# Attention maxima split into three parts before the turn instead of after it, in a one-core transformer block

## The reference, cut to what matters

```
q, k, v = layernorm(x) @ w_qkv, split into heads
scores = q k^T / sqrt(8), causal mask (-inf above the diagonal)
scores += head_scale * (q . dir) * (k . dir)
attn = softmax(scores)           # over the keys
x = x + layernorm((attn v) @ w_out)
```

## Time and profile before

| what | us |
|---|---|
| runs | 540.02, 540.23 (median), 547.24 |
| profiled execution, span from first to last instruction | 542.4 |
| TensorE busy | 440.5 (81%) |
| VectorE busy | 329.6 (61%) |
| ScalarE busy | 244.3 (45%) |
| GpSimd busy | 142.2 (26%) |
| mean granted TensorE clock | 0.899 |

### The profile page before, as it was taken

How to read it: one execution, slowest core, us unless ns; L and a number is a source line. 1 busy time by engine, 2 the same in 40 slices (tenths; PEclk the granted TensorE clock), 3 DMA queues, 4 the chain that set the end, 5 groups by cost and what they waited for, 6 DMA issues and landing times. The chain is left out here.

```text
span 542.4 us, 10816 instructions
## 1 busy us (share of the span) xinstructions
PE 440.5 (81%) x3980; PEld 267.0 (49%) x3980; DVE 329.6 (61%) x885; ACT 244.3 (45%) x432; POOL 142.2 (26%) x211
## 2 busy tenths in 40 slices
PE   1845978989898998999898968888699989898800
PEld 0522432434434352434434345645499889888800
DVE  3975956868787876878782764599223322223356
ACT  1520145666665765677675827552122222213330
POOL 9300000010111101011111002424626665573423
PEclk9975576999989997999988988999979999999965
DMA  3065254100202020000000008100447768766352
GB/s 102 21 179 150 78 157 119 58 5 3 60 2 61 2 60 2 2 3 3 3 2 2 1 2 232 39 2 1 160 137 228 205 194 215 215 206 190 98 160 78
DMA packets 44616, 46.60 MB, mean 86 GB/s; under 512 B 6355, under 2 KB 33364, under 8 KB 44564
## 3 DMA queue, kind: packets, MB, share of 16 engines
q1 hardware_dynamic: 42132, 40.92, 25.8%
q0 software_dynamic: 2432, 4.99, 3.6%
HBM read 34.80 MB, written 10.88 MB: 84 GB/s over the span
## 5 line engine op out<-in xcount | busy, mean ns | idle before, releaser
L611 ACT ACTIVATE probs<-banks 128x1024 f32<-128x1024 f32 (+1 forms) x192 | 145.3, 810 | 80.6 <-PE banks L468 52.5
L749 DVE TENSOR_REDUCE mx_part<-banks 128x1 f32<-128x512 f32 (+3 forms) x256 | 133.2, 584 | 42.1 <-PE banks L444 34.2
L444 PE MATMUL banks<-k_st,q_st 48*128 48x512 bf16 (+3 forms) x384 | 123.9, 370 | 14.5 <-DMA k_st<-k_rows 12.3
L461 PE MATMUL banks<-q_st,k_st 51*128 51x512 bf16 (+3 forms) x384 | 103.7, 349 | 17.7 <-DMA q_st<-mx_rows 11.3
L480 PE MATMUL banks<-probs,v_pad 128*32 128x512 f32 (+3 forms) x768 | 86.8, 526 | 0.0
L461 PEld LDWEIGHTS banks<-q_st,k_st 51*128 51x128 bf16 x384 | 32.1, 96 | 75.7 <-ACT probs L611 49.9
L749 DVE TENSOR_REDUCE mx<-banks 128x1 f32<-128x512 f32 (+3 forms) x128 | 54.7, 485 | 20.1 <-PE banks L450 20.0
L1488 DVE TENSOR_TENSOR hidden<-banks,gate 128x512 f32<-128x512 f32 x38 | 26.3, 692 | 61.6 <-ACT gate L1256 28.8
L355 POOL TENSOR_TENSOR mx_rest<-mx_neg,mx_rows 16x128 f32<-16x128 f32 x16 | 6.7, 417 | 199.2 <-ACT mx_neg L621 199.2
L444 PEld LDWEIGHTS banks<-k_st,q_st 48*128 48x128 bf16 x384 | 34.7, 95 | 43.6 <-DVE mx_part L749 24.8
L448 PE MATMUL banks<-mask_qk,ident_half 64*128 64x128 bf16 x256 | 56.2, 232 | 0.0
(11 more groups left out here) (198 smaller groups left out, 616.1 us busy)
## 6 DMA issues: line engine op xcount, KB each, us to landing
w_g<-in_w_gate SPq DMA_DIRECT2D x38, 256.0 KB
w_u<-in_w_up SPq DMA_DIRECT2D x38, 256.0 KB
q_rows<-parts SPq DMA_DIRECT2D x24, 128.0 KB, 2.4
k_rows<-parts SPq DMA_DIRECT2D x24, 128.0 KB, 2.4
q_st<-q_rows SPq DMA_DIRECT2D x32, 96.0 KB, 2.3
k_st<-k_rows SPq DMA_DIRECT2D x32, 96.0 KB, 2.3
w_d<-in_w_down SPq DMA_DIRECT2D x8, 256.0 KB, 4.9
back<-results SPq DMA_DIRECT2D x8, 256.0 KB, 4.8
```

What stands on the lines that cost most here:

```text
L444: last = nc.tensor.matmul(dst[:, 0:width], q_st[r][rows, c, p, (i % CH) * P:(i % CH + 1) * P], k_st[r][rows, kc, p, 0:width], start=True, ...
L461: last = nc.tensor.matmul(dst[a][:, 0:width], k_st[r][rows, j // CH, p, (j % CH) * P:(j % CH + 1) * P], q_st[r][rows, c, p, first:BANK], s ...
L611: nc.scalar.activation(probs[unit % PROBS][:, 2 * p:2 * p + 2, first:BANK], slot_pair[k % 2].rearrange("p (a t) -> p a t", a=2)[:, :, 0:BA ...
L749: nc.vector.tensor_reduce(dst, max_bank[m % RING][:, 0:width], AX.X, ALU.max, negate=True).then_inc(max_taken, 1)
```

## The change

GpSimd now splits the maxima while they still lie in the partitions (128 x 16 numbers, four instructions) into `mx_split`, 48 bf16 columns in the order half, part, head and block. TensorE turns all 48 with one bf16 product against an identity. ScalarE copies 48 rows once and thereby frees the slot. SyncE issues two transfers of three rows each. The four entries in the hand-written orders (rows of (n, 1), outputs of (n - 1, 1), rows of (n + 1, 0), outputs of (n, 0)) each stand one unit later.

```
-            if x == 0:
+            if x == 1:
                 slots.append(("rows", n, 1))
-            if x == 1 and n > 0:
+            if x == 2 and n > 0:
                 slots.append(("out", n - 1, 1))
-            if x == 5 and n + 1 < GROUPS:
+            if x == 6 and n + 1 < GROUPS:
                 slots.append(("rows", n + 1, 0))
-            if x == 6:
+            if x == 7:
                 slots.append(("out", n, 0))
...
             def send_rows(n, c):
-                sp.wait_ge(rows_split, n * NC + c + 1)
+                sp.wait_ge(slot_taken, SLOT_AT["rows", n, c] + 1)
                 for a in range(2):
-                    for part in range(3):
-                        row = a * HALF + KR + part
-                        sp.dma_start(q_st[n % STACKS][row:row + 1, c, :, :].rearrange("o p t -> o (p t)"),
-                                     mx_rows[c][n % 2][a * 2 * CH:(a + 1) * 2 * CH, part, :]
-                                     ).then_inc(rows_ready[c], 16)
+                    row = a * HALF + KR
+                    sp.dma_start(q_st[n % STACKS][row:row + 3, c, :, :].rearrange("o p t -> o (p t)"),
+                                 mx_rows[c][n % 2][a * 6 * CH:(a + 1) * 6 * CH, :]
+                                 ).then_inc(rows_ready[c], 16)
...
             def split_rows(n, c, count):
-                pool.wait_ge(high_row_ready, 2 * (n * NC + c + 1))
-                high, mid, low = (mx_rows[c][n % 2][:, i, :] for i in range(3))
-                nc.gpsimd.tensor_tensor(mx_rest[c][:, :], mx_neg[c][:, :], high, ALU.subtract
-                                        ).then_inc(pool_steps, 1)
+                if c == 0:
+                    pool.wait_ge(max_taken, n * MAXIMA + CH * HG)
+                else:
+                    pool.wait_ge(max_merged, n + 1)
+                whole = mx[c][n % 2][:, :].rearrange("p (a m) -> p a m", a=2)
+                rest = mx_rest[c][:, :].rearrange("p (a m) -> p a m", a=2)
+                high, mid, low = (mx_split[c][n % 2][:, :, i, :] for i in range(3))
+                nc.gpsimd.tensor_copy(high, whole).then_inc(pool_steps, 1)
                 pool.wait_ge(pool_steps, count + 1)
-                nc.gpsimd.tensor_copy(mid, mx_rest[c][:, :]).then_inc(pool_steps, 1)
+                nc.gpsimd.tensor_tensor(rest, whole, high, ALU.subtract).then_inc(pool_steps, 1)
                 pool.wait_ge(pool_steps, count + 2)
-                nc.gpsimd.tensor_tensor(low, mx_rest[c][:, :], mid, ALU.subtract).then_inc(rows_split, 1)
+                nc.gpsimd.tensor_copy(mid, rest).then_inc(pool_steps, 1)
+                pool.wait_ge(pool_steps, count + 3)
+                nc.gpsimd.tensor_tensor(low, rest, mid, ALU.subtract).then_inc(rows_split, 1)
...
             def turn_maxima(n, c):
                 dst = free_slot(("rows", n, c))
-                if c == 0:
-                    pe.wait_ge(max_taken, n * MAXIMA + CH * HG)
-                else:
-                    pe.wait_ge(max_merged, n + 1)
-                nc.tensor.transpose(dst[0][:, 0:P], mx[c][n % 2][:, :], ident[:, :]).then_inc(slot_filled, 1)
+                pe.wait_ge(rows_split, n * NC + c + 1)
+                nc.tensor.matmul(dst[0][0:3 * HG * CH, 0:P], mx_split[c][n % 2][:, :, :, :].rearrange("p a r m -> p (a r m)"),
+                                 ident_b[:, :], start=True, stop=True).then_inc(slot_filled, 1)
...
             def take_rows(n, c):
                 k = SLOT_AT["rows", n, c]
                 act.wait_ge(slot_filled, k + 1)
-                src = slot_bank[k % 2][0][0:HG * CH, 0:P]
-                nc.scalar.activation(mx_rows[c][n % 2][:, 0, :], src, ACT.Copy).then_inc(high_row_ready, 1)
-                nc.scalar.activation(mx_neg[c][:, :], src, ACT.Copy).then_inc(high_row_ready, 1)
-                act.wait_ge(high_row_ready, 2 * (n * NC + c + 1))
-                act.sem_inc(slot_taken, 1)
+                nc.scalar.activation(mx_rows[c][n % 2][:, :], slot_bank[k % 2][0][0:3 * HG * CH, 0:P], ACT.Copy
+                                     ).then_inc(slot_taken, 1)
```

More of the change, by code:

```diff
@@ L171, in program @@
         mx_part = [sb_front(f"mx_part{i}", [P, HG * CH, 2]) for i in range(2)]
[L172 to L175, removed]
+        mx = [[sb_front(f"mx{c}{i}", [P, HG * CH]) for i in range(2)] for c in range(NC)]
+        mx_rest = [sb_front(f"mx_rest{c}", [P, HG * CH]) for c in range(NC)]
+        mx_split = [[sb_front(f"mx_split{c}{i}", [P, 2, 3, 2 * CH], BF16) for i in range(2)] for c in range(NC)]
+        mx_rows = [[sb_front(f"mx_rows{c}{i}", [3 * HG * CH, P], BF16) for i in range(2)] for c in range(NC)]
+        ident_b = sb_front("ident_b", [P, P], BF16)
         probs = [sb_front(f"probs{i}", [P, HG, BANK]) for i in range(PROBS)]
@@ L220, in program @@
         max_merged = sem("max_merged")
-        high_row_ready = sem("high_row_ready")
         rows_split = sem("rows_split")
@@ L346, in _ @@
             pool.wait_ge(consts_ready, 1 + 12)
-            for c in range(NC):
-                for i in range(2):
-                    nc.gpsimd.memset(mx[c][i][:, :], 0.0).then_inc(consts_ready, 1)
+            nc.gpsimd.affine_select(out=ident_b[:, :], in_=zeros_b[:, :], compare_op=ALU.not_equal, fill=1.0,
+                                    base=0, pattern=[[-1, P]], channel_multiplier=1).then_inc(consts_ready, 1)
             def split_rows(n, c, count):
-                pool.wait_ge(high_row_ready, 2 * (n * NC + c + 1))
-                high, mid, low = (mx_rows[c][n % 2][:, i, :] for i in range(3))
-                nc.gpsimd.tensor_tensor(mx_rest[c][:, :], mx_neg[c][:, :], high, ALU.subtract
-                                        ).then_inc(pool_steps, 1)
+                if c == 0:
[6 more added lines that the diff above has]
+                nc.gpsimd.tensor_copy(high, whole).then_inc(pool_steps, 1)
                 pool.wait_ge(pool_steps, count + 1)
-                nc.gpsimd.tensor_copy(mid, mx_rest[c][:, :]).then_inc(pool_steps, 1)
+                nc.gpsimd.tensor_tensor(rest, whole, high, ALU.subtract).then_inc(pool_steps, 1)
                 pool.wait_ge(pool_steps, count + 2)
-                nc.gpsimd.tensor_tensor(low, mx_rest[c][:, :], mid, ALU.subtract).then_inc(rows_split, 1)
+                nc.gpsimd.tensor_copy(mid, rest).then_inc(pool_steps, 1)
+                pool.wait_ge(pool_steps, count + 3)
+                nc.gpsimd.tensor_tensor(low, rest, mid, ALU.subtract).then_inc(rows_split, 1)
             def normalise(n, c):
@@ L377, in _ @@
             for n in range(GROUPS):
-                split_rows(n, 1, steps + 4 * n + 2)
+                split_rows(n, 1, steps + 6 * n + 3)
                 if n > 0:
@@ L381, in _ @@
                 if n + 1 < GROUPS:
-                    split_rows(n + 1, 0, steps + 4 * n + 4)
+                    split_rows(n + 1, 0, steps + 6 * n + 6)
                 normalise(n, 0)
@@ L459, in score @@
                 if p == 0 and a == 0 and x in (0, CH):
-                    pe.wait_ge(rows_ready[c], 16 * 6 * (n + 1))
+                    pe.wait_ge(rows_ready[c], 16 * 2 * (n + 1))
                 last = nc.tensor.matmul(dst[a][:, 0:width],
@@ L537, in _ @@
             pe.wait_ge(v_stored, 4)
-            pe.wait_ge(consts_ready, 1 + 12 + 4)
+            pe.wait_ge(consts_ready, 1 + 12 + 1)
             for x in range(UNITS):
@@ L541, in _ @@
                     maxima(0, x, p, a, s)
-                if x == 5:
+                if x == 6:
                     turn_maxima(0, 0)
@@ L643, in _ @@
                         exponentials(n, x, p)
-                    if x == 0:
-                        if n > 0:
-                            take_sums(n - 1, 1)
+                    if x == 0 and n > 0:
+                        take_sums(n - 1, 1)
+                    if x == 1:
                         take_rows(n, 1)
-                    if x == 1 and n > 0:
+                    if x == 2 and n > 0:
                         take_outputs(n - 1, 1)
@@ L735, in invert_sums @@
                                      ).then_inc(sums_inverted, 1)
-            dve.wait_ge(consts_ready, 1 + 12 + 4)
+            dve.wait_ge(consts_ready, 1 + 12 + 1)
             for n in range(GROUPS):
```

## The result

| | median us | lowest to highest | runs |
|---|---|---|---|
| before | 543.25 | 540.02 to 547.24 | 4 |
| changed | 526.0 | 523.35 to 528.47 | 4 |

The ratio is 0.9697, with a 95% interval of 0.9652 to 0.9743: 14 to 19 us less. The profiled span fell from 542.4 to 524.4 us, by 18.0. The forecast was 527.4. It was worked out from a median of 540.2 for the kernel before, which is 543.25 over these four runs: the time came within 1.4 us of the forecast, while the gain, 17.25 us, was 4.5 more than the 12.8 forecast.

A forecast was written before the change was run, and what follows sets the result against it. It took TensorE's waits for late row transfers at unit 4 (11.3 us) to bound the kernel, each at full length. Terms 6.2 + 4.4 + 2.1 + 0.6 - 0.5 = 12.8 us off 540.2 gave 527.4, range 522 to 534.

The forecast's parts named there:

- the clock's rival: TensorE's short stretches at 1.2 GHz in attention all go; gain 18.3 us, about 522 us, chance 0.06.
- Direction and bound: TensorE's waits for row transfers at unit 4, 11.3 us in 7 waits, each cost their full length.
- Groups 1 to 6, 6.2 us: At unit 4 the rows land in time with 0.3 to 1.3 us margin; all waits go, 6.2 us gained.
- Group 0, 4.4 us: At unit 4 the rows release at 78.9, wanted at 78.2; of 5.13 us waiting 0.7 stays, 4.4 gained.
- The shape of the transfers, 0.16 us: Three-row transfers from 24 partitions take 0.16 us, between nothing and 0.5, fitting in the margin.
- GpSimd, nothing: GpSimd's four split instructions take 1.2 us, covered between VectorE's merge and TensorE's turn; cost nothing.
- The slot, 2.1 us: ScalarE frees the slot after one copy, not two and a wait; 2.1 us gained, between nothing and 4.
- VectorE's new wait, -0.5: VectorE's reciprocals at units 3 and 8 wait for the output just copied; 0.5 us lost, at most 3.5.
- The clock, 0.6 us: Less time at 1.2 GHz on TensorE, counted for group 0 alone; 0.6 us gained.
- Given back: Unit 4 waits go, but the slot gains nothing and each VectorE reciprocal costs 0.25; about 533 us, chance 0.21.
- rows still late: Three-row transfers land 1.5 us later than 0.16, so 5.7 of the 12.8 return; about 534 us, chance 0.07.
- slower: TensorE's turn waits for GpSimd's split once its four instructions take over 5 us; about 551 us, chance 0.04.

The follow-up runs named there:

- the kernel with only the shorter way: Kernel before with split ahead of the turn, one product and one copy, but old units and six one-row transfers; 534.0 us, ratio 0.9801.
- the kernel with the old units: Changed kernel with the turns and copies of rows and outputs back at units 0, 1, 5 and 6; 525.91 us, ratio 0.9724.
- the kernel with six transfers: Changed kernel with its two three-row transfers cut into six of one row, later units kept; 550.49 us, ratio 1.0155.

## Why the prediction was right, and where a size was off

*The time.* It was right, and in part by luck. The gain was 4.5 us larger than forecast, in the profiled run mostly for the clock (below), and the time still came near, as the median that it was counted from, 540.2, was 3.05 us below that of the four runs. By its gain, 17.25 us in the medians and 18.0 in the spans, the case came nearer to the clock's rival (18.3) than to the forecast (12.8).

*Direction and bound.* Right. The waits at unit 4 reach the end, and without them groups 1 to 5 take the same time to 0.01 us. But a wait costs 0.17 us more than its length. In the kernel with only the shorter way, group 1 took 29.82 with its wait of 0.91 and groups 2 and 3 took 28.74 and 28.73 without one; unit 3 alone went from 1.68 to 2.76. In the kernel before, groups 1 to 6 all had a wait, so the difference of two of them could not show this, and the 29.0 that I took for a group without a wait still holds these 0.17.

*Groups 1 to 6, 6.2 us.* Right: all gone, and with the 0.17 of each wait they were worth 7.2. The margin, given as 0.3 to 1.3, is 0.9. The release 6.21 us after the first issue in group 1, which I took as the worst case without asking why, goes with an instruction packet among the last rows.

*Group 0, 4.4 us.* The release was put at 78.9 and came at 78.83. But TensorE wanted the rows at 77.0, not 78.2, as attention began 1.0 earlier and units 0 to 3 together were 0.2 shorter. 1.8 us of waiting stayed instead of 0.7, and the group gained 3.2.

*The shape of the transfers, 0.16 us.* Slightly low. Release follows the first issue by 2.89 instead of 2.7. The second issue starts 0.81 after the first, where one-row transfers start 0.69 apart, and release follows the last issue's start by 2.08 instead of 1.80, so 0.28 is the later landing. The Trainium skill's rule on the number of engines (DMA: Bandwidth & Descriptors, section on why a DMA increments its semaphore by 16) points the same way. The trace does not name the engines, but its packets are in keeping with eight and three: a one-row transfer has 16, eight of them the rows' 256 bytes, and a three-row one 27, 24 of them such rows, so eight and three are left over.

*GpSimd, nothing.* Right: four instructions of 0.20 to 0.22 us, 1.1 in all, where I took 1.2, with 3.7 to spare.

*The slot, 2.1 us, and VectorE's new wait, -0.5.* Groups 1 to 6 are 0.33 us shorter each, 2.0 in all, near the 1.6 that the two terms make together, but half of that is not the slot. 0.17 belongs to the waits, as above. The way to the transfers as a whole gives about 0.1 (28.84 to 28.73), the later units 0.06 more, with VectorE's new wait already in it. A second copy costs nothing (28.66), so one copy in place of two is worth nothing by itself. Whether the bf16 product in place of the float32 turn or ScalarE's wait that fell away makes the 0.1 was not told apart. VectorE's wait was a sign of being wrong by my own list (over 0.3 each time), and it came: 0.59 and 1.16 us. It costs 0.17 per group, 1.2 us over seven groups (an estimate from groups 1 to 6), where I took 0.5.

*The clock, 0.6 us.* This is the term that was mis-sized. I gave the short stretches no gain since the last of them had no wait before it. The 0.6 itself, for group 0, did not come: its stretch fell from 10.2 to 6.8 us, but units 4 to 11 took 21.7 us where they had taken 20.9. In the profiled run all four went: group 2 is 1.1 shorter for it (30.71 - 0.59 - 29.0), group 4 1.7 (32.06 - 1.35 - 29.0), group 6 1.1 (30.44 - 0.61 - 28.7, its last unit being 0.3 shorter than the others'), and about 1.0 of group 7's 1.9 lies there too, as its unit 1 took 3.55 before and 2.52 in the kernel with the old units: 4.9, about 5 us. The two kernels with and without the eight products show that waits can bring the lower clock. They are not its only cause: single stretches without a wait came in the old-order kernel, in that with two copies and in one profile of the changed kernel (group 5, 29.97 us). Why those come stays open. The clock's rival, 522 at a chance of 0.06, thus named what the profiled run did to the groups.

*Given back; rows still late; slower.* None came. The first has its measured price in the reciprocals, about 1.2 us in all against the 3.5 of that rival.

## What to carry to other kernels

Where one engine waits for a transfer of a few kilobytes, count the issues ahead of it on its queue: here each took 0.62 to 0.75 us with one row (2 KB) and 0.70 to 0.88 with three (6 KB), and the last of them sets the landing. Parts that shorten one path share one margin, so try each both alone and with the others: here a reordering cost 16 us or nothing, depending on the transfers. And price a wait of TensorE with the clock that may follow it; with six transfers and the later units that doubled the cost.

## What was not expected of the hardware

In groups 1 to 6 of the kernel with six transfers, waits of 1.85, 1.21, 2.24, 1.57, 1.21 and 1.23 us at unit 4 were each followed by 6.8 us at 1.2 GHz, at a cost of about 1.7 us each. In the kernel before, waits of 1.65 and 1.43 us were followed by none. Shorter waits did so in part: in the kernel with only the shorter way, of 0.91 (group 1) and 0.94 us (group 4), a stretch at 1.2 GHz followed the second alone, and group 4 took 31.55 us. Eight products with no use, 512 columns each, in front of the same wait kept the clock at 2.4 GHz and made the kernel 8 us faster. In six of the profiled groups a single packet of 8 or 16 KB from the instruction queue, overlapping the last rows, went with a landing 0.8 to 1.8 us later than usual.
